# Token stage of a state-space and expert layer: 512 tokens as the moving side, downs a group later, selection in pieces

## What is computed

```python
# layer norm, 4-tap convolution and projection to 16 states, scan over time
h = associative_scan(A_bar, B_bar)               # [4, 2048, 16]
x1 = x + (C * h) @ Wout + b_out                  # what the token stage starts from
xn = layernorm(x1)                               # its output rows go to the experts
scores = sigmoid(xn @ w_router)                  # [tokens, 64]
# 8 groups of 8 experts: sum of the two best each, best 4 groups, in them the best 8 experts
topk_w = 2.5 * s / sum(s)
y = sum over the 8 experts of w * (silu(xn @ we_gate) * (xn @ we_up)) @ we_down
shared = (silu(xn @ ws_gate) * (xn @ ws_up)) @ ws_down      # ws_*: 512 to 256 to 512
out = x1 + y + shared
```

## Time and profile before

| | |
|---|---|
| median of 3 executions | 3753.27 us (3749.15 to 3755.29) |
| the profiled execution | 3752.3 us, span 3750.6 us, granted clock 0.973 |
| busy share of the span | PE 93%, PEld 77%, DVE 63%, ACT 37%, POOL 46% |
| first and last instruction of the token stage | 223.3 to about 697 us |

### The profile page before, as it was taken

One profiled execution on the slowest core, in us unless ns is written; L12 is line 12 of the kernel. 1 busy time (PEld: TensorE's weight loads), 2 busy tenths in 40 slices (PEclk: granted clock), 3 DMA queues, 4 the chain that ended last, 5 costly groups with the idle time before them and its releaser, 6 DMA issues.

```text
span 3750.6 us, 111626 instructions
## 1 busy us (share of the span) xinstructions
PE 3506.6 (93%) x17368; PEld 2883.6 (77%) x17369; DVE 2344.7 (63%) x5897; ACT 1404.4 (37%) x4167; POOL 1720.7 (46%) x1372
## 2 busy tenths in 40 slices
PE   7659999399999999999999999999999999999996
PEld 5548888288787888878888788888888888888885
DVE  6578887555666656566556655666565666656553
ACT  5624444133333434343333433333333334333331
POOL 1202121145555555555555555555555555555543
PEclk9879999699999999999999999999999999999998
DMA  5423333256676666676666766676666677667654
GB/s 161 116 79 125 123 127 103 70 118 138 149 153 152 156 130 157 124 172 142 139 129 141 166 124 130 141 159 125 143 125 126 141 171 162 141 126 168 132 102 73
DMA packets 217557, 502.66 MB, mean 134 GB/s; under 512 B 47504, under 2 KB 47632, under 8 KB 217114
## 3 DMA queue, kind: packets, MB, share of 16 engines
q0 software_dynamic: 129024, 320.94, 45.5%
q1 hardware_dynamic: 85434, 176.04, 14.1%
q10 hardware_dynamic: 3040, 5.03, 0.5%
HBM read 1115.79 MB, written 191.41 MB: 349 GB/s over the span
## 4 chain that ended last, share of the span: by engine, by line
PE 69%; issue 4%; DMA 3%; DVE 2%; DVEq 1%; ACT 1%; ACTq 1%; POOLq 0%; SPq 0%; POOL 0%
PE e_ps_gu L1674 39%; PE e_ps_y L1693 19%; PE e_ps_x L1643 6%; PE e_ps_h L1703 3%; DMA out<-e_y,e_y_ids 3%; PE e_ps_find L1656 1%; DVE e_w_low L1817 1%; ACT e_w_high L1754 0%; DVEq L1525 0%; DMA e_w_raw<-in_L_ffn_we_down 0%; DVE e_below L1860 0%; ACTq L1525 0%; ACT e_xT_high L1762 0%; DVE e_y L1844 0%; DVE e_xT_low L1825 0%
## 5 line engine op out<-in xcount | busy, mean ns | idle before, releaser
L1605 POOL DMA_INDIRECT out<-e_y,e_y_ids x576 | 982.7, 1706 | 1238.3 <-SPq L1575 581.7
L1597 POOL DMA_INDIRECT e_x<-token_rows,e_x_ids x576 | 612.7, 1064 | 213.9 <-issue 168.7
L1674 PE MATMUL e_ps_gu<-e_w_high,e_xT_high 128*128 x2304 | 681.0, 417 | 17.3 <-issue 9.8
L1674 PE MATMUL e_ps_gu<-e_w_high,e_xT_low 128*128 x2304 | 635.7, 398 | 0.0
L1674 PE MATMUL e_ps_gu<-e_w_low,e_xT_high 128*128 x2304 | 634.4, 397 | 0.0
L1773 ACT ACTIVATE e_silu<-e_ps_gu 128x256 f32<-128x256 f32 x576 | 221.3, 384 | 1008.9 <-PE e_ps_gu L1674 872.5
L1825 DVE TENSOR_TENSOR e_xT_low<-e_ps_x,e_xT_high 128x512 fp32r<-128x512 f32 x576 | 397.4, 690 | 270.4 <-ACT e_xT_high L1762 129.5
L1844 DVE TENSOR_SCALAR e_y<-e_ps_y,e_weight 128x512 f32 (+1 forms) x576 | 430.8, 748 | 215.7 <-PE e_ps_y L1693 181.9
L1674 PEld LDWEIGHTS e_ps_gu<-e_w_high,e_xT_low 128*128 128x128 f32 x2304 | 435.5, 189 | 107.0
L1674 PEld LDWEIGHTS e_ps_gu<-e_w_low,e_xT_high 128*128 128x128 f32 x2304 | 434.0, 188 | 103.4
L1837 DVE TENSOR_TENSOR e_h<-e_silu,e_ps_gu 128x256 f32<-128x256 f32 x576 | 240.4, 417 | 377.9 <-ACT e_silu L1773 307.5
(11 more groups left out here) (300 smaller groups left out, 4245.8 us busy)
## 6 DMA issues: line engine op xcount, KB each, us to landing
e_w_raw<-in_L_ffn_we_gate SPq DMA_DIRECT2D x576, 512.0 KB
e_w_raw<-in_L_ffn_we_up SPq DMA_DIRECT2D x576, 512.0 KB
e_w_raw<-in_L_ffn_we_down SPq DMA_DIRECT2D x576, 512.0 KB
a_x<-in_L_attn_x SPq DMA_DIRECT2D x64, 256.0 KB, 2.7
t_x_in<-in_L_attn_x SPq DMA_DIRECT2D x64, 256.0 KB, 2.8
token_rows<-t_xn SPq DMA_DIRECT2D x64, 256.0 KB, 2.0
out<-t_y_out SPq DMA_DIRECT2D x64, 256.0 KB, 2.0
e_x<-token_rows,e_x_ids POOLq DMA_INDIRECT x576
```

What stands on the lines that cost most here:

```text
L1597: pool.indirect_dma_start(x[:, s % XS, :], None, k.rows, bass.IndirectOffsetOnAxis(x_ids[:, s:s + 1], 0)) \
L1605: pool.indirect_dma_start(k.out, bass.IndirectOffsetOnAxis(y_ids[:, s:s + 1], 0), y[:, s % YS, :], None, compute_op=ALU.add).then_inc(adde ...
L1674: last = nc.tensor.matmul(ps_gu[s % 2][:], x[:, s % 2, c, :], w[:, c], start=(n == 0), stop=(n == 3 * DC - 1))
```

## The change

In `token_tiles` the roles of the operands change. A group's four tiles are turned and split into one buffer of 512 tokens per group (`xT_high`, `xT_low`, two halves for two groups). `gate_up(g, half, n, first, to)` is one of four sweeps n (gate or up, first or second 128 hidden columns), with a piece of weight [128 x 128] stationary and 512 tokens moving; a sweep has 12 matmuls and may be cut into parts. Gate has one bank (`ps_gate`), up one (`ps_up`), so the next gate sweep waits for silu, the next up sweep for h. h comes out as hidden x tokens, so it is split as it is, and `turn_h` is gone. The router's weights are split into high and low and stacked as 128 columns (`w_r_parts`); 8 matmuls make the two parts of the scores, transposed; `keep_r` copies them, and `fold` adds both parts and turns them back in four products with a stacked identity. `ps_x` has two banks, the copy for the router is gone, xn has one buffer instead of two. The steps are new: downs of group g - 1 in step 1 of g, each followed by a scan output of g + 1 and by a third of the first gate sweep; `choose` is cut into `take_top` and `strike`, which stand between residuals; `count` is two groups behind.

```diff
@@ shared weights: layout of ws_down; split and stacked router weights
-            act.dma_start(k.w_down[:], k.ws_down.rearrange("(p c) d -> p c d", c=FC)).then_inc(k.shared_loaded, 16)
+            act.dma_start(k.w_down[:], k.ws_down.rearrange("(c p) d -> p c d", p=P)).then_inc(k.shared_loaded, 16)
...
+            nc.gpsimd.tensor_tensor(k.fold[:], k.ident[:, 0:E], k.ident[:, E:P], ALU.add)
+            pool.wait_ge(w_high_ready, 5)
+            nc.gpsimd.tensor_tensor(k.w_r_parts[:, :, E:2 * E], k.w_r[:], k.w_r_parts[:, :, 0:E].bitcast(F32),
+                                    ALU.subtract)
...
+            nc.scalar.copy(k.w_r_parts[:, :, 0:E], k.w_r[:]).then_inc(w_high_ready, 1)
...
@@ tensor engine
-                pe.wait_ge(xT_low_ready, i + 1)
-                chunks = xn[:, half, s, :].rearrange("p (q c) -> p c q", c=DC)
+                after(pe, xT_low_ready, i - 1)
+                chunks = xn[:, s, :].rearrange("p (q c) -> p c q", c=DC)
                 for c in range(DC):
-                    last = nc.tensor.transpose(ps_x[:, c, :], chunks[:, c, :], k.ident[:])
+                    last = nc.tensor.transpose(ps_x[s % 2][:, c, :], chunks[:, c, :], k.ident[:])
                 last.then_inc(xt_done, 1)
 
-            def gate_up(g, s, turned):
-
-
-                i = SUB * g + s
-                pe.wait_ge(xT_high_ready, i + 2)
-                pe.wait_ge(h_made, i + 1)
-                for j, (x, w) in enumerate(((xT_high, k.w_gu_high), (xT_high, k.w_gu_low), (xT_low, k.w_gu_high))):
-                    if x is xT_low:
-                        if turned:
-                            turn_h(*turned)
-                        pe.wait_ge(xT_low_ready, i + 2)
+            def gate_up(g, half, n, first=0, to=3 * DC):
+
+
+                j, fc = n % 2, n // 2
+                bank = (ps_gate, ps_up)[j]
+                if first == 0:
+                    pe.wait_ge(xT_high_ready, SUB * (g + 1))
+                    after(pe, (silu_made, hT_made)[j], FC * g + fc)
+                passes = [(x, w, c) for x, w in ((xT_high, k.w_gu_high), (xT_high, k.w_gu_low), (xT_low, k.w_gu_high))
+                          for c in range(DC)]
+                for i in range(first, to):
+                    x, w, c = passes[i]
+                    if i == 2 * DC:
+                        pe.wait_ge(xT_low_ready, SUB * (g + 1))
+                    last = nc.tensor.matmul(bank[:], w[:, j, c, P * fc:P * fc + P], x[:, half, c, :], start=(i == 0),
+                                            stop=(i == 3 * DC - 1))
+                if to == 3 * DC:
+                    last.then_inc(gu_done, 1)
+
+            def route(g, half):
+                after(pe, scored, g)
+                pe.wait_ge(xT_high_ready, SUB * (g + 1))
+                for i, x in enumerate((xT_high, xT_low)):
+                    if i == 1:
+                        pe.wait_ge(xT_low_ready, SUB * (g + 1))
                     for c in range(DC):
-                        last = nc.tensor.matmul(ps_gu[s % 2][:], x[:, s % 2, c, :], w[:, :, c, :],
-                                                start=(j == 0 and c == 0), stop=(j == 2 and c == DC - 1))
-                last.then_inc(gu_done, 1)
-
-            def route(g, s):
-                i = SUB * g + s
-                pe.wait_ge(xT_ready, i + 2)
-                pe.wait_ge(scored, i + 1)
-                for c in range(DC):
-                    last = nc.tensor.matmul(ps_r[:, s, :], xT[:, s % 2, c, :],
-                                            k.w_r[:, c, :], start=(c == 0), stop=(c == DC - 1))
+                        last = nc.tensor.matmul(ps_rT[:], k.w_r_parts[:, c, :], x[:, half, c, :],
+                                                start=(i == 0 and c == 0), stop=(i == 1 and c == DC - 1))
+                last.then_inc(rT_done, 1)
...
+            def fold(g):
+                pe.wait_ge(rT_kept, g + 1)
+                for s in range(SUB):
+                    last = nc.tensor.matmul(ps_r[:, s, :], rT[:, P * s:P * s + P], k.fold[:], start=True, stop=True)
...
+            def down(g, half, s):
+                after(pe, out_made, SUB * g + s)
+                pe.wait_ge(hT_high_ready, FC * (g + 1))
...
+            def down_and_residual(g, half, s, behind, ahead):
+                if behind >= 1:
+                    down(g - 1, 1 - half, s)
+                if ahead >= 1:
+                    ssm_out(g + 1, 1 - half, s)
             def step(g, half, s, behind, ahead):
+                if s == 0:
+                    if behind >= 1:
+                        gate_up(g - 1, 1 - half, 3, 0, 6)
+                    turn_x(g, half, 2)
+                    if behind >= 1:
+                        gate_up(g - 1, 1 - half, 3, 6)
+                    turn_x(g, half, 3)
+                    if ahead >= 1:
+                        ssm_out(g + 1, 1 - half, 0)
+                    if behind >= 2:
+                        count(g - 2, half)
+                elif s == 1:
+                    route(g, half)
+                    if behind >= 1:
+                        down(g - 1, 1 - half, 0)
+                    for t in range(1, SUB):
+                        gate_up(g, half, 0, DC * (t - 1), DC * t)
+                        down_and_residual(g, half, t, behind, ahead)
+                elif s == 2:
+                    gate_up(g, half, 1)
+                    fold(g)
                 else:
+                    gate_up(g, half, 2)
+                    if ahead >= 1:
+                        for t in range(2):
+                            turn_x(g + 1, 1 - half, t)
...
@@ scalar engine
             def step(g, half, s, behind, ahead):
+                if s == 0:
+                    if behind >= 1:
+                        sigmoid(g - 1, 1)
+                    keep_x(g, half, 2)
+                    keep_x(g, half, 3)
+                    if behind >= 1:
+                        keep_h(g - 1, 1 - half, 1)
+                elif s == 1:
+                    keep_r(g)
+                    if behind >= 2:
+                        keep_counts(g - 2, half)
+                    if ahead >= 2:
+                        copy_states(g + 2, half)
+                    sigmoid(g, 0)
+                elif s == 2:
+                    if ahead >= 1:
+                        normalize(g + 1, 1 - half, 0)
+                    score(g, half)
+                    if ahead >= 1:
+                        normalize(g + 1, 1 - half, 1)
+                    keep_h(g, half, 0)
                 elif ahead >= 1:
+                    normalize(g + 1, 1 - half, 2)
+                    for t in range(2):
+                        keep_x(g + 1, 1 - half, t)
+                    normalize(g + 1, 1 - half, 3)
...
@@ vector engine
+            def gated(g, fc):
+                v.wait_ge(sig_ready, FC * g + fc + 1)
+                after(v, hT_high_ready, FC * g + fc)
+                nc.vector.tensor_tensor(hT[:], sig[:], ps_gate[:], ALU.mult).then_inc(silu_made, 1)
+
+            def hidden(g, fc):
+                v.drain()
+                v.wait_ge(gu_done, 2 * FC * g + 2 * fc + 2)
+                nc.vector.tensor_tensor(hT[:], hT[:], ps_up[:], ALU.mult).then_inc(hT_made, 1)
+
+            def keep_h_low(g, half, fc):
+                v.wait_ge(hT_high_ready, FC * g + fc + 1)
+                after(v, o_done, SUB * (g - 1))
+                nc.vector.tensor_tensor(hT_low[:, half, fc, :], hT[:], hT_high[:, half, fc, :].bitcast(F32),
...
+            def next_rows(g, half, s, behind, ahead):
+                if behind >= 1:
+                    finish(g - 1, 1 - half, s)
+                    v.drain()
+                if ahead >= 1:
+                    residual(g + 1, 1 - half, s)
+
             def step(g, half, s, behind, ahead):
+                if s == 0:
+                    if behind >= 1:
+                        gated(g - 1, 1)
+                    keep_low(g, half, 2)
+                    if behind >= 1:
+                        hidden(g - 1, 1)
+                    keep_low(g, half, 3)
+                    if behind >= 1:
+                        keep_h_low(g - 1, 1 - half, 1)
+                        open_groups()
+                elif s == 1:
+                    for t in range(SUB):
+                        next_rows(g, half, t, behind, ahead)
+                        if ahead >= 1:
+                            spread(g + 1, 1 - half, (t,))
+                        if t == 0 and behind >= 1:
+                            take_top()
+                        elif t == 1 and behind >= 1:
+                            strike(g - 1, 1 - half)
+                        elif t == 2:
+                            gated(g, 0)
+                    if ahead >= 1:
+                        variance()
+                elif s == 2:
+                    hidden(g, 0)
+                    if ahead >= 1:
+                        shifts(g + 1)
+                else:
                     group_halves(g, half)
+                    keep_h_low(g, half, 0)
```

(5 more changed lines are left out.)

295 lines of the change are left out of this document (94 added, 201 removed).

## The result

| | kernel before | changed kernel |
|---|---|---|
| median of the runs | 3750.2 us (3749.15 to 3755.29) | 3767.5 us (3765.86 to 3768.85) |
| ratio, 95% interval | 1 | 1.0042, 1.0028 to 1.0057 |
| profiled span | 3750.6 us | 3764.2 us |
| rstd of group 1, of group 15 | 250.89, 629.89 | 252.52, 637.83 |
| period of a group | 27.07 us | 27.52 us (25.6 to 26.5 predicted) |

The change is slower by 0.42%, and 3735 us were predicted. So two things want an explanation: a token stage that ends 6.65 us later and not 17 earlier, and an expert stage that is 7.3 us longer with the same instructions. That is 13.6 us between the two profiled spans. The medians differ by 17.3, since the profiled execution of the kernel before (3752.3 us) took 2.1 us more than its median and that of the changed kernel (3765.86) 1.6 less.

A forecast was written before the change was run, and what follows sets the result against it. TensorE bounds now, VectorE would after: 24.0 us work plus 2.05 waits, 26.05 a group for 27.07. 14 x (27.07 - 26.05) = 14.3, plus 4, minus 1.4: 17 us off 3752.3, so 3735 us (own range 3725 to 3744; chance 0.56).

The forecast's parts named there:

- The total is 24.0 us: VectorE's work per group of 512 tokens in the new token stage, summed over its steps; before, 24.2 us at most.
- The waits: VectorE's waits for rstd 0.45, scores 1.2, xT_low 0.3 and hT_low 0.1 us, added to its work: 2.05 a group.
- step 0: VectorE's gate times sigmoid, two xT_low, hidden, hT_low and opening the groups: 5.53 us a group.
- step 1: VectorE's four outputs, residuals and statistics, with masking, top-8, strike, one gate product, variance and a drain: 12.9 us a group.
- steps 2 and 3: VectorE's hidden, shift, group maxima, hT_low, two xT_low and group scores: 5.5 us a group.
- The rule on drains: Skill page that would make VectorE's added drains free; the forecast priced five at 0.17 us, leaving free drains 2 in 100.
- Rival C: VectorE's queue between variance and group scores: old waits of 2.9 us stay, 28.55 us a group, 3771 us; chance 0.11.
- Start and end: Token stage's start loses 1.4 us (0 to 4); its end, 41.5 us from last rstd to last output, saves 4.
- The expert stage computes the same in both kernels: Stage behind the token stage: unchanged, so a microsecond saved in the token stage is one saved in the span.

The follow-up runs named there:

- e2: Changed kernel with GpSimd's weights of the group before started only behind VectorE's shift; 26.72 us a group, 3754.03 us, ratio 1.0002 to the kernel before.
- e4: Changed kernel with each output put between the residual of the tile before and its drain, three drains fewer a group; 3747.39 us, ratio 0.9986 to the kernel before.
- e6: Changed kernel with outputs and residuals in turn, GpSimd's weights behind the shift, and scores ahead of normalized tiles; 3734.49 us, ratio 0.9943 to the kernel before.
- e1: Changed kernel with ScalarE's scores ahead of the normalize of tile 0 instead of behind it; 3759.92 us, ratio 1.0019 to the kernel before.
- e13: The changed kernel, unaltered, run again on another chip; 3767.13 us, ratio 1.0034 to the kernel before.
- e15: The kernel of e6, unaltered, run again on another chip; 3731.83 us, ratio 0.9941 to the kernel before.

## Why the prediction was wrong

**Step that failed: "The total is 24.0 us", VectorE's work in a group.** The waits were right (2.0 for 2.05), TensorE waits for VectorE as forecast, and the period was 27.52 for 26.05. By the rows shown above, part by part:

| part | predicted | measured | rows |
|---|---|---|---|
| step 0 | 5.53 | 5.80 | 535.55 to 541.35 |
| step 1 | 12.9 | 13.40 | 541.35 to 554.75 |
| steps 2 and 3, less waits | 5.5 | 6.47 | 527.23 to 535.55, less 0.36 + 1.28 + 0.21 |
| work | 24.0 | 25.67 | |

- 0.84 us are the two collisions with GpSimd, in steps 2 and 3; the other 0.13 of their 0.97 is spread over small steps. The prediction priced VectorE's order alone. The change also brought GpSimd's weights right behind rstd, where the shift waits. e2 put them behind the shift, nothing else, and got 0.80 back.
- 0.5 us are in step 1. Its terms as named add up to 13.0, not 12.9, so 0.1 is a slip of addition. The rest is the step from output to residual, for which I took the drained pace, 0.77: the first and third take 0.95 and 0.91 here. The rows of before had 0.92 (571.67 to 572.59) with 0.23 idle "<-PE t_ps_y", and I struck that idle as a wait for TensorE that would go. It stayed, under another name ("issue", 0.23 to 0.27), four times a group. e4 takes three of them out, with the drains beside them, and got 0.97 back.
- Step 0 has the remaining 0.3: hidden starts 0.78 behind xT_low (536.14 to 536.92) where I had one such step at 0.60, and opening the groups took 2.27 (539.08 to 541.35) for 2.19.

**The rule on drains.** The sentence of the Trainium skill that I went against ("VectorE: DVE Perf Modes", "The DRAIN you can't avoid") would have made added drains free. That reading was too strong: the same section goes on that a next operation that isn't held starts earlier, and 0.60 us from start to start in operations of 0.69 agrees with that. The experiments speak against free drains once more: with three drains fewer and the same work, e4's group is 0.97 us shorter. What I missed was in the other direction: a residual behind a drain starts 0.91 to 0.95 us behind its output, not 0.77. A drain with a wait that is already met does not explain it, for hidden has both and starts 0.78 behind xT_low (536.14 to 536.92). The residual also has a second wait and a register instruction ahead of it; without a drain before it, in e4, it has them too and starts 0.61 behind (538.87 to 539.48). Which of them costs the 0.15 behind a drain wasn't tried.

**Rival C** named the slower side and the right place, VectorE's queue, but not the mechanism. Its price was 2.9 us of old waits that stay; waits measured 2.0. It would have decided at 3.25 us of waits a group. What decided instead was 1.7 us of work. That its time, 3771 us, lies near the 3767.5 measured is luck: the period it gives is 28.55 us for 27.52, and 7.3 us come from a stage that it held constant.

**Start and end.** The start lost 1.63 us (252.52 - 250.89) for 1.4. At the end I had the last output 41.5 us behind the last rstd; it came 682.51 - 637.83 = 44.7 behind, for 45.8 before: 1.1 saved, not 4. The same mis-sized work stands in that sum.

**"The expert stage computes the same in both kernels"** was true and didn't help. Its length is not a constant of its instructions: 3026.7 to 3036.4 us in the seventeen profiles of the table. 7.3 us of the 13.6 us of span are this, and their cause stays open. With 13 or 27 drains the changed kernel is 5.3 and 6.4 us slower than the kernel before (3752.59 x 0.0014 and x 0.0017), which its token stage alone would explain: 6.65 us, and 0.7 to 1.4 for the drains.

**The balance.** The forecast moved the stage end by 17 us to the front, the trace by 6.65 to the back, a miss of 23.65. The period makes 14 x 1.47 = 20.6 of it, the start 0.2, the end 2.7. The expert stage adds 7.3, and the profiled execution lies 1.6 us below the median (3764.2 + 1.7 for 3767.5). That makes 32.4 of the 32.5 that were measured, 3767.5 - 3735.

## What to carry to other kernels

Where the engine that sets the pace is changed, look at what its neighbours issue at the same moment: here a small operation of VectorE beside one of GpSimd took four times its time, and one wait on GpSimd's side brought it back. Idle time of 0.2 us ahead of an operation that follows a drain may stay when its named releaser is gone; let one drain serve two producers, as e4 does. When a kernel's largest stage is untouched, measure it all the same, and run the kernels that are compared on one chip before a loss of 0.2% is put down to the change.

## What the runs showed of the hardware

- The same 128x4 operation of VectorE took 156 to 164 ns alone (before, e2, e6) and 630 beside a 128x256 fp32 operation of GpSimd; a 128x32 one 184 and 562, a 128x128 one 293 and 609 (e6). All of these read both operands from SBUF. A 128x512 one with an operand in PSUM stayed at 0.69 us beside the same operation of GpSimd (585.99, before).
- An output, residual and statistics, with the gate product behind them, took 2.30 us with a drain between output and residual, and 1.96 with one drain for two tiles (e4), each operation itself unchanged at 0.67 to 0.69.
- The expert stage, with the same instructions, took 3034.6 to 3036.4 us in some kernels and 3029.0 to 3030.3 in others on the same chips (e1 and e2 against e4, e13 against e15). One program took 3034.2 us on one chip and 3030.3 on another.
